# Layer 3's scores as one two-column matmul, spread by transposes: a four-layer graph network on one core

## The reference

```python
Wh = jnp.einsum('bnf,fo->bno', h, W)
a1, a2 = (a[:Fout, 0], a[Fout:, 0])
s1 = Wh @ a1
s2 = Wh @ a2
e = s1[:, :, None] + s2[:, None, :]
e = jnp.where(e >= 0, e, ALPHA * e)
e = jnp.where(adj_matrix[None] == 0, -jnp.inf, e)
attention = jax.nn.softmax(e, axis=-1)
h_prime = jnp.einsum('bij,bjo->bio', attention, Wh)
```

## Time and profile before

| | |
|---|---|
| runs | 656.16, 659.46, 662.39 us (median 659.46) |
| span of the profiled execution | 655.8 us |
| busy, share of that span | PE 87%, PEld 78%, DVE 75%, ACT 51%, POOL 29% |
| one step of the loop (start of `hidden1` at 423.56, 472.35, 521.09 us) | 48.8 us |
| PEclk by slices, in tenths | 9 in every slice from 262 to 606 us, 7 in the last three |

### The profile page before, as it was taken

One profiled execution on the slowest core, in us unless ns is written; L12 is line 12 of the kernel. 1 busy time (PEld: TensorE's weight loads), 2 busy tenths in 40 slices (PEclk: granted clock), 3 DMA queues, 4 the chain that ended last, 5 costly groups with the idle time before them and its releaser, 6 DMA issues.

```text
span 655.8 us, 11662 instructions
## 1 busy us (share of the span) xinstructions
PE 573.3 (87%) x3890; PEld 513.5 (78%) x3890; DVE 490.2 (75%) x1398; ACT 333.4 (51%) x594; POOL 192.6 (29%) x216
## 2 busy tenths in 40 slices
PE   2999795788788939999999999899999999899763
PEld 1888443688777939898999899899899899799653
DVE  5588587788899583448669869869869869766885
ACT  1566781686765503334563563563563553642660
POOL 7640610121112250404404504404404305213220
PEclk9999798798999968999999999999999999999777
DMA  6323001111210000000000100100100100100002
GB/s 172 91 70 96 1 0 31 34 32 39 58 33 1 0 1 1 0 2 0 1 1 1 33 0 0 32 0 0 32 0 0 32 0 0 32 1 23 11 0 64
DMA packets 28382, 15.27 MB, mean 23 GB/s; under 512 B 2320, under 2 KB 28048, under 8 KB 28352
## 3 DMA queue, kind: packets, MB, share of 16 engines
q1 hardware_dynamic: 27792, 13.65, 7.2%
q0 software_dynamic: 560, 1.25, 0.7%
HBM read 10.69 MB, written 4.19 MB: 23 GB/s over the span
## 4 chain that ended last, share of the span: by engine, by line
PE 34%; DVE 19%; issue 9%; ACT 3%; POOL 3%; DVEq 1%; POOLq 0%; ACTq 0%
PE psum L224 7%; PE psum L226 7%; PE psum L225 7%; DVE ob L218 4%; PE psum L1498 4%; DVE ln_st L183 3%; DVE keep_x L218 2%; ACT soft L1173 2%; PE psum L1450 2%; PE psum L1440 2%; POOL ln_r L200 2%; DVE soft L854 1%; DVE keep_x L811 1%; DVE ln_ag L188 1%; DVE ext_lo L878 1%
## 5 line engine op out<-in xcount | busy, mean ns | idle before, releaser
L200 POOL TENSOR_TENSOR ln_r<-ln_v,mhalf 128x8 f32<-128x8 f32 x24 | 39.6, 1649 | 282.4 <-DVE ln_v L194 282.4
L1154 ACT ACTIVATE h<-psum 128x512 f32<-128x512 f32 x64 | 38.3, 598 | 49.7 <-PE psum L226 49.7
L1498 PE MATMUL psum<-l2w_s,h 128*128 128x128 f32 x512 | 59.6, 275 | 0.0
L1498 PEld LDWEIGHTS psum<-l2w_s,h 128*128 128x128 f32 x512 | 59.0, 192 | 0.7
L218 DVE TENSOR_SCALAR keep_x<-keep_x,ln_ag,ln_r 128x128 f32<-128x128 f32 (+1 forms) x128 | 50.0, 467 | 4.1 <-POOL ln_r L200 4.1
L224 PE MATMUL psum<-qt_hi,l2w_s_hi 128*128 128x512 f32 x128 | 52.4, 410 | 0.0
L226 PE MATMUL psum<-qt_hi,l2w_s_lo 128*128 128x512 f32 x128 | 50.5, 394 | 0.0
L225 PE MATMUL psum<-qt_lo,l2w_s_hi 128*128 128x512 f32 x128 | 50.4, 393 | 0.0
L832 DVE SCALAR_TENSOR_TENSOR h_lo<-psum,h_hi 128x1024 fp32r<-128x1024 f32 x16 | 19.6, 1224 | 35.8 <-ACT h_hi L1145 35.8
L466 POOL COPY keep_x<-x1r 128x512 f32 (+1 forms) x16 | 16.3, 1020 | 88.0 <-DVE x1r L218 88.0
L1173 ACT ACTIVATE soft<-soft,s1c 128x256 f32<-128x256 f32 x64 | 26.8, 497 | 29.8 <-DVE m L854 29.7
(11 more groups left out here) (244 smaller groups left out, 1950.7 us busy)
## 6 DMA issues: line engine op xcount, KB each, us to landing
xin<-in_x SPq DMA_DIRECT2D x64, 128.0 KB, 2.3
out_x<-ob SPq DMA_DIRECT2D x32, 128.0 KB, 1.9
l2w_raw<-in_l2w POOLq DMA_DIRECT2D x1, 512.0 KB, 5.5
adjs<-in_adj SPq DMA_DIRECT2D x1, 256.0 KB, 2.8
adjs<-in_adj_t SPq DMA_DIRECT2D x1, 256.0 KB, 3.0
l2w_s<-in_l2w POOLq DMA_DIRECT2D x1, 256.0 KB, 5.1
w_raw<-in_w_t SPq DMA_DIRECT2D x1, 128.0 KB, 3.2
w2t<-in_w_t SPq DMA_DIRECT2D x1, 128.0 KB, 3.2
```

The costliest lines, as they stand in the source:

```text
L200: pool.tensor_tensor(ln.r[:].rearrange("p s k -> p (s k)"), ln.v[:].rearrange("p s k -> p (s k)"), mhalf[:], ALU.pow).then_inc(ln.rstd, 1)
L1154: act.activation(h2[:, s, g, :], bank(4 + g)[:, 0, :], ACT.Relu).then_inc(h2_out, 1)
L1498: i = pe.matmul(bank(s)[:, 0, k * D:(k + 1) * D], h2[:, s, g, j * N + t * P:j * N + (t + 1) * P], l2w3_s[:, g, :], start=(g == 0), stop=(g ...
```

## The change

The four one-column matmuls become four two-column matmuls against all of `wa`, which write s1 and s2 of each node into bank 6 + s; a new semaphore `s12_done` tells DVE. DVE first copies the eight columns of both slots into `s12` in SBUF. The 512-column matmul, `wa2_bc` and its POOL instruction are gone. In their place a new PE function `spread3` waits for DVE's copy (`s1_out`) and transposes, four times a slot, the s2 column of `s12`, broadcast to 128 columns, into bank 4 + s; now this tells DVE by `s2_done`. `spread3` of both slots stands between `mix_out(p, 0)` and `mix_out(p, 1)`, and in the tail behind `attend3(IT - 2, 1)`.

```diff
         wa = sb("wa", [P, 2])
-        wa2_bc = sb("wa2_bc", [P, P])
...
-            pool.tensor_scalar(wa2_bc[:], ones[:], wa[:, 1:2], None, ALU.mult).then_inc(wa2_ready, 1)
...
             def scores3(p):
 
                 for s in range(2):
-                    q = 2 * p + s
-                    dve.wait_ge(s2_done, q + 1)
-                    dve.tensor_copy(s1c[:, s, :], bank(6 + s)[:, 0, 0:4]).then_inc(s1_out, 1)
+                    dve.wait_ge(s12_done, 2 * p + s + 1)
+                    dve.tensor_copy(s12[:, s].rearrange("p k c -> p (k c)"), bank(6 + s)[:, 0, 0:8]).then_inc(s1_out, 1)
+                for s in range(2):
+                    wait_apart(dve, dc, s2_done, 2 * p + s + 1)
                     for k in range(4):
...
-                        pe.matmul(bank(6 + s)[:, 0, k:k + 1], xt3[:, s, j * N + t * P:j * N + (t + 1) * P], wa[:, 0:1],
-                                  start=True, stop=True)
-                pe.matmul(bank(4 + s)[:, 0, :], wa2_bc[:], xt3[:, s, :], start=True, stop=True).then_inc(s2_done, 1)
+                        i = pe.matmul(bank(6 + s)[:, 0, 2 * k:2 * k + 2], xt3[:, s, j * N + t * P:j * N + (t + 1) * P], wa[:],
+                                      start=True, stop=True)
+                i.then_inc(s12_done, 1)
+
+            def spread3(p, s):
+
+                pe.wait_ge(s1_out, 2 * p + s + 1)
+                for j in range(2):
+                    for t in range(T):
+                        c = j * N + t * P
+                        i = pe.transpose(bank(4 + s)[:, 0, c:c + P], s12[:, s, 2 * t + j, 1:2].broadcast_to([P, P]), ident[:])
+                i.then_inc(s2_done, 1)
...
-                for s in range(2):
-                    mix_out(p, s)
+                mix_out(p, 0)
+                if behind:
+                    for s in range(2):
+                        spread3(p - 1, s)
+                mix_out(p, 1)
...
             attend3(IT - 2, 1)
+            for s in range(2):
+                spread3(IT - 1, s)
```

More of the change, by code:

```diff
@@ L131, in build @@
         picked, a_edge_done, log_ready = sem("picked"), sem("a_edge_done"), sem("log_ready")
-        weights_split, wgt_ready, wa2_ready = sem("weights_split"), sem("wgt_ready"), sem("wa2_ready")
+        weights_split, wgt_ready = sem("weights_split"), sem("wgt_ready")
         bst1 = sb("bst1", [P, H0 // P, Q, 6])
@@ L247, in build @@
         x3_ready, t3_done, xt3_out = sem("x3_ready"), sem("t3_done"), sem("xt3_out")
-        s2_done, s1_out, tm_done, m_step = sem("s2_done"), sem("s1_out"), sem("tm_done"), sem("m_step")
+        s12_done, s2_done, s1_out, tm_done, m_step = sem("s12_done"), sem("s2_done"), sem("s1_out"), sem("tm_done"), sem("m_step")
         zt_ready, lk_ready, ex_ready = sem("zt_ready"), sem("lk_ready"), sem("ex_ready")
@@ L309, in build @@
         m3 = sb("m3", [P, 2, 4])
-        s1c = sb("s1c", [P, 2, 4])
+        s12 = sb("s12", [P, 2, 4, 2])
+        s1c, s2c = s12[:, :, :, 0], s12[:, :, :, 1]
         zm = sb("zm", [P, 3, 2, 4])
@@ L860, in scores3 @@
                 dve.wait_ge(s1_out, 2 * p + 2)
-                dve.tensor_tensor(zm[:, 0], m3[:], s1c[:], ALU.add).then_inc(m_step, 1)
+                dve.tensor_tensor(zm[:, 0], m3[:], s1c, ALU.add).then_inc(m_step, 1)
                 dve.wait_ge(m_step, 3 * p + 1)
@@ L1172, in sum_scores @@
                     for k in range(4):
-                        i = act.activation(soft[:, s, k, :], soft[:, s, k, :], ACT.Identity, bias=s1c[:, s, k:k + 1])
+                        i = act.activation(soft[:, s, k, :], soft[:, s, k, :], ACT.Identity, bias=s12[:, s, k, 0:1])
                     i.then_inc(zt_ready, 1)
@@ L1641, in _ @@
             step(0, first=True, behind=False, two_behind=False, beside=last_attention)
-            pe.wait_ge(wa2_ready, 1)
             step(1, two_behind=False)
```

## The result

The changed kernel takes 677.66 us in the median (673.15 to 681.19, 4 runs) against 659.99 us (656.16 to 662.39, 4 runs) of the kernel before; the ratio is 1.0271, with a 95% interval of 1.0237 to 1.0305. The time forecast was 669.5 us, the range 662 to 677: the direction was right, the size too small, and the median lies 0.7 us above the range. The profiled execution took 677.35 us, of which its span is 675.3 us.

The account below looks back on a forecast made before the run. The prediction took DVE's chain up to PE's hidden1 to bound the loop; 4.4 + 1.45 + 2 x 1.44 = 8.7 us on 659.5 gave 668.2, plus 1.3 for one clock fall 669.5 us, range 662 to 677 us.

Parts of the forecast that it names:

- DVE is the path in the loop, PE waits: Loop steps: DVE's sums lead through ACT to PE's hidden1, setting step length; PE has 1.59 us to spare.
- The second column, the wider copy and PE's saved work are worth nothing: Loop: two columns cost nothing; PE's net gain of 1.03 us a step only lengthens its idle time.
- The stall of 0.88 us a pass: Loop, between DVE's copy and first sum: DVE waits for the s2 transposes; five passes, 4.4 us.
- Step 1, step 7 and the tail: There mix_out or attend3 and the round trip precede the first sum: +1.45, +1.44 and +1.44 us.
- The clock: PE from hidden1 on: longer idle time drops it to half clock; one extra fall counted, 1.3 us.
- the likeliest case: Whole kernel: stall and later sums plus one extra clock fall, 669.5 us; 666 to 673 us, chance 0.49.
- falls in nearly every pass: Rival, loop: clock falls 4 to 5 times, 5 to 9 us on top, 673 to 677 us; chance 0.27.
- the sum of the other terms, 8.7 us: Whole kernel without the clock: 4.4 us in five passes, 1.45 in step 1, 2 x 1.44 in step 7 and tail.
- A covered stall: Rival, whole kernel: stall partly covered, sum 6.5 us or less, 662 to 666 us; chance 0.2.
- PE as the path: Rival, every step: PE sets the length, its 1.03 us a step is gained, 8.2 us, 651 us; chance 0.04.

Follow-up runs that it names:

- before_delay: Kernel before with two extra, unused mask reductions on DVE (about 0.9 us) ahead of scores3 in every step with scores; 670.36 us, ratio 1.0141.
- two_columns: Kernel before with two-column score matmuls and DVE copying eight columns, second column unused, 512-column matmul kept; 657.74 us, one run.
- early_copy: Changed kernel with DVE's two score-column copies moved ahead of the last two norm3 operations in steps 2 to 7; 671.31 us, ratio 1.0179.
- after_filler: Changed kernel with twelve extra PE matmuls ahead of hidden1's wait for pt_lo, in every step but the first; 672.38 us, ratio to kernel before 1.0172.
- spread_first: Changed kernel with both slots' transposes ahead of both mix_out groups instead of between them; 666.89 us, one run.
- reworked: Changed kernel with early copies, transposes ahead of mix_out (tail: ahead of attend3(6, 1)) and twelve extra matmuls ahead of hidden1; 665.40 us, ratio 1.0076.

## Why the prediction was wrong, point by point

**DVE is the path in the loop, PE waits.** Right; `before_delay` shows it directly, 0.92 us on DVE alone made the pass without a fall 1.0 us longer (step 2, 49.7 against 48.7).

**The second column, the wider copy and PE's saved work are worth nothing.** Right in the loop (`two_columns`). PE's saving looks worse than nothing, since it became idle time: in `early_copy` the stall is gone, and the wait ahead of `hidden1` is 2.4 us all the same, 0.8 us more than before, near the 1.0 us of work that PE no longer has; the clock fell there in three of five passes. No run takes this work away and changes nothing else.

**The stall of 0.88 us a pass.** Right in steps 2 to 5: 0.78 us of waiting, and 49.6 to 49.8 us a pass in `after_filler`, 0.8 to 1.0 us more than before. (PE idled 0.59 us ahead of the transposes, where I had 0.9.) For step 6 it was too small, 1.3 us: I had read one pass and taken five as alike, but in step 6 DVE has less to do and meets PE in `mix_out`. All five: 4.9 us against 4.4.

**Step 1, step 7 and the tail.** The mechanism was right, the sizes a little low. Who waited for the transposes, in us and times:

```profile
  DVE soft L853: 10.7, 8
```

These are 8 waits of 10.7 us together, where there had been 3.5 us. Step 1 is 1.7 us longer (1.45 forecast). From the first score matmul to the last sum step 7 took 6.79 us against 5.23, 1.56 longer (1.44 forecast), and the tail 7.68 against 5.30, 2.4 longer (1.44 forecast):

```profile
643.98 1.91 PE L1535 MATMUL psum<-ident,s 128*128 128x128 f32 x8
```

```profile
645.18 0.42 DVE L853 CUSTOM_DVE_ANT_0 soft<-psum,mask 128x256 f32<-128x256 f32 x1 [2.69 <-PE psum L1535]
```

The tail's transposes ran at half clock, 1.91 us in place of 1.09. Part of that comes back behind them; from step 7 on the net is 3.6 us against 2.9. `spread_first` shows the cause in step 1: with nothing ahead of the transposes it is back at 41 us. Behind that the cause is in part argued: in `reworked`, with the tail's transposes moved too, the rest is back at 87.5 us, but the copies, the twelve matmuls and the stretches at half clock differ as well, and the four kernels whose transposes stand where the changed kernel has them, with nothing added in the tail, lie anywhere from 90.9 to 92.6 us.

**The clock: the step that failed.** The prediction named the mechanism and the place, "1.6 us is at the edge in this kernel, and the changed one idles 2.47 us there" (measured 2.39), and priced a fall at 1.3 us (measured 1.4 to 1.6). It then counted "one such fall more than before as part of the likeliest case" and gave falls in nearly every pass 0.27. The profiled execution has five: four begin within 0.1 us of the start of `hidden1` in steps 3 to 6, the fifth 0.8 us behind it in step 7. The four cost 6.4 us in the passes. With the sum of the other terms, 8.7 us, that is 15.1 us, on the median 659.5 + 15.1 = 674.6 us, inside the rival's 673 to 677 us. What failed is the term for the clock, one fall of 1.3 us where the passes had four of 1.6 us: the reason given against more, that the profiled execution before had no fall, was a statement about waits of 1.6 us, and the wait had grown by half. Why the clock fell in these passes and not in step 2, behind the same wait, stays open. The remaining 1.5 us of the change's 16.6 are 0.3 us in step 1, 0.5 in step 6 and 0.7 from step 7 on.

**The two other rivals.** A covered stall and PE as the path are both excluded by the passes of 49.6 us in `after_filler` against 48.8.

## What to carry to other kernels

A wait that ends a step can cost more than its own length when TensorE sits behind it: price the delay, then ask how long TensorE idles with it and what the stretch behind would cost at half clock. In `reworked` the clock fell behind waits under 1 us too, so read the granted clock of every pass rather than trust one length of wait. Work taken from an engine that already waits does not help, and on TensorE it can cost; a replacement by smaller operations that go through another engine adds a round trip exactly where the old, larger one was ready in time. And read every pass of a loop, the last above all, before multiplying one pass's number by their count.

## What the runs showed of the hardware

- The same idle time of TensorE, 2.4 us, was followed by a fall of the clock in some passes and not in others (`early_copy`, 427.66 and 476.51; the changed kernel at 330.60, with 2.40 us, without one). At 1.5 to 1.7 us ahead of `hidden1` there was none in the loop of any kernel; with 12 short matmuls in the wait (0.9 us idle) none at the `hidden1` of steps 2 to 6. But `reworked` had falls at its transposes behind 0.79 and 0.93 us.
- Where the pass is near 51.2 us the falls repeat in every pass: in the changed kernel they begin at 380.4, 431.6, 482.8, 534.0 and 585.2 us, in `before_delay` at 379.6, 430.8, 482.0 and 533.2, each 51.2 us apart, and the passes settle at 51.1 to 51.4 us. In `early_copy`, whose passes are shorter, two of five passes escape. What ties the two together was not tested.
- 3.4 us at half clock cost 1.4 to 1.6 us of a pass where PE was the path behind it (`early_copy`, 50.29 against 48.85 us; the changed kernel, 51.2 against 49.6 in `after_filler`).
- A transpose of a column broadcast by stride 0 took as long as one of a full tile: in the changed kernel 273 ns median in both (L1535 and L1516), 0.11 us apart.
